# Routing tokens to slots of one expert each in a two-layer transformer kernel on one NeuronCore

## What is computed

```python
xn = _layernorm(x)
probs = softmax(einsum('bsd,ed->bse', xn, Wr))
topv, topi = top_k(probs, 2)
combine = sum(topv[..., None] * one_hot(topi, 8), axis=2)
for e in range(8):                       # w1: 128 x 512, w2: 512 x 128
    h = gelu(einsum('bsd,dh->bsh', xn, w1[e]) + b1[e])
    out += combine[..., e, None] * (einsum('bsh,hd->bsd', h, w2[e]) + b2[e])
x = x + attention0(xn) + out
...
```

## Time and profile before

| | us |
|---|---|
| median of 3 runs (lowest, highest) | 2019.29 (2015.37, 2021.03) |
| the profiled execution's own time | 2017.26 |
| its span in the profile | 2015.5 |
| TensorE busy | 1758.9 (87%) |
| VectorE, ScalarE, GpSimd busy | 1471.3, 1327.4, 654.6 |

### The profile page before, as it was taken

How to read it: one execution, slowest core, us unless ns; L and a number is a source line. 1 busy time by engine, 2 the same in 40 slices (tenths; PEclk the granted TensorE clock), 3 DMA queues, 4 the chain that set the end, 5 groups by cost and what they waited for, 6 DMA issues and landing times. The chain is left out here.

```text
span 2015.5 us, 36012 instructions
## 1 busy us (share of the span) xinstructions
PE 1758.9 (87%) x10163; PEld 1049.0 (52%) x10163; DVE 1471.3 (73%) x4707; ACT 1327.4 (66%) x2819; POOL 654.6 (32%) x1554
## 2 busy tenths in 40 slices
PE   5899999999998897999858889888888838888877
PEld 2455555577776443566524555555555525555544
DVE  5588888311123464888668999999999879999974
ACT  3277777544331522334378999999999839999983
POOL 2154544300002451000044443544354414434440
PEclk8699999999995997999879999999999969999978
DMA  6300000100001221000110110111011101101000
GB/s 163 95 25 20 23 23 16 44 1 0 0 2 49 79 89 42 0 0 0 45 32 17 33 33 17 32 32 32 16 32 32 32 1 32 32 16 32 22 18 15
DMA packets 38186, 61.76 MB, mean 31 GB/s; under 512 B 10226, under 2 KB 15348, under 8 KB 38005
## 3 DMA queue, kind: packets, MB, share of 16 engines
q1 hardware_dynamic: 38069, 60.51, 10.2%
HBM read 34.14 MB, written 17.83 MB: 26 GB/s over the span
## 5 line engine op out<-in xcount | busy, mean ns | idle before, releaser
L1655 ACT ACTIVATE a_trash<-a_sc,a_search 128x1024 bf16<-128x1024 f32 (+7 forms) x768 | 586.1, 767 | 67.4 <-POOL a_search L1591 31.0
L1405 PE MATMUL a_ps_s<-a_k,a_q 128*128 128x512 f32 (+3 forms) x768 | 310.3, 519 | 57.6 <-DVE a_sc L1871 51.5
L1439 PE MATMUL a_ps_o<-a_kT,a_v 128*65 128x512 f32 (+3 forms) x768 | 288.1, 499 | 54.3 <-ACT a_kT L1672 52.7
L1423 PE MATMUL a_ps_t<-g_ident,a_sc 128*128 128x128 f32 x1152 | 227.6, 284 | 19.5 <-ACT a_kT L1672 18.1
L1871 DVE TENSOR_SCALAR_CACHE_REDUCE a_sc<-a_ps_s,g_search 128x1024 f32<-128x1024 f32 (+7 forms) x256 | 207.8, 812 | 25.5 <-PE a_ps_s L1407 17.3
L593 DVE TENSOR_REDUCE a_top<-a_ps_row 128x1 f32<-128x512 f32 (+3 forms) x384 | 196.7, 553 | 26.3 <-PE a_ps_row L431 20.3
L1831 DVE SCALAR_TENSOR_TENSOR a_below<-a_sc,a_found 128x768 f32<-128x768 f32 (+7 forms) x256 | 211.3, 835 | 1.1
L1405 PEld LDWEIGHTS a_ps_s<-a_k,a_q 128*128 128x128 f32 x768 | 131.9, 196 | 153.6 <-issue 93.1
L1425 PE MATMUL a_ps_t<-a_minus,a_short 128*128 128x128 bf16 x1152 | 211.1, 221 | 0.0
L1423 PEld LDWEIGHTS a_ps_t<-g_ident,a_sc 128*128 128x128 f32 x1152 | 164.0, 142 | 90.0 <-ACT a_kT L1672 46.1
L557 ACT ACTIVATE a_prob<-a_ps_col 128x1024 f32<-128x1024 f32 (+7 forms) x256 | 159.2, 650 | 68.9 <-PE a_ps_col L444 65.6
(11 more groups left out here) (267 smaller groups left out, 3382.0 us busy)
## 6 DMA issues: line engine op xcount, KB each, us to landing
a_v<-g_v SPq DMA_DIRECT2D x32, 260.0 KB, 2.3
q1turned<-p_full SPq DMA_DIRECT2D x32, 256.0 KB, 2.0
a_q<-q1turned SPq DMA_DIRECT2D x32, 256.0 KB, 3.6
a_k<-k1turned SPq DMA_DIRECT2D x32, 256.0 KB, 4.0
stack<-p_parts SPq DMA_DIRECT2D x24, 256.0 KB, 3.7
le_q<-stack SPq DMA_DIRECT2D x32, 96.0 KB, 2.2
le_k<-stack SPq DMA_DIRECT2D x32, 96.0 KB, 2.2
le_w<-d_w SPq DMA_DIRECT2D x1, 2048.0 KB, 9.4
```

What stands on the lines that cost most here:

```text
L1405: pe.matmul(ps_s[:, j % 2, c:c + w], q[:, p, i * P:width], k[:, p, c:c + w], start=True, stop=True)
L1423: pe.matmul(out, columns(h, i)[:, c * P:(c + 1) * P], g.ident[:, :], is_transpose=True, start=True, stop=False)
L1439: m = pe.matmul(ps_o[0:VW1, lo // HALF, (lo % HALF) * P:CH], v[:, p, c, :], kT[:, u % 2, a * P:b * P], start=(c == 0), stop=(c == LAST[lo ...
L1655: act.activation(trash[:, u % 2, 0:(i + 1) * P], columns(h, i), ACT.Sign, scale=-1.0, bias=trials[:, p, c, i:i + 1], accum_out=balance[:, ...
```

## The change

Each token takes two experts, so 4096 pairs of token and expert are left. They are sorted by expert into slots of 128 rows; a slot belongs to one expert, and the number of slots, NSLOT = 39, is the most that any routing can need. All 39 are always computed.

The router's matmuls move between the query products, and VectorE picks experts, ranks the tokens and works out each token's two rows (`g.spot`) and each slot's expert (`g.owner`) between its copies of values. In attention, SP first fills a buffer in memory with zeros; GpSimd, in sections 4 to 19, sends each tile of `xn` there twice by indirect DMA, each token's row to its place. In the experts' stage SP reads the slots back, and per slot TensorE transposes the 128 rows, VectorE copies them, GpSimd copies the owner's `w1` to a ring of four buffers, ScalarE takes four Gelus of 128x128, and TensorE reads `w2` at an address from a register. TensorE, ScalarE and GpSimd each load the slot's owner from memory on chip into a register. VectorE copies results, and SP saves three slots at a time. In `project_layer1` GpSimd gathers two rows per token by 32 indirect DMAs, ahead of its memsets, and VectorE adds them times the token's two probabilities. The addition of `g.acc` is gone. GpSimd's sections of attention are written out instead of looped. The four bias operations stand between the slots' copies, after slots 18, 22, 26 and 30.

```diff
+NSLOT = (2 * B * S + NE * (P - 1)) // P
+GS = 3
...
+                pool.memset(taken[:, 0:LEAD, :], 0.0).then_inc(lead_clear, 1)
+                pool.memset(sums[:, :, 0:LEAD, :], 0.0).then_inc(lead_clear, 1)
+                pool.memset(ends[:, :, 0:NE // 2], 0.0).then_inc(lead_clear, 1)
+                pool.memset(g.zero[:, :], 0.0).then_inc(lead_clear, 1)
+                pool.wait_ge(lead_clear, 4)
...
+                def choose():
+
+                    dve.wait_ge(r_ready, 1)
+                    dve.wait_ge(w_in, 16 * 15)
+                    dve.wait_ge(lead_clear, 4)
+                    keep(dve.tensor_copy(g.logits[:, :, :], ps_r[:, :, :]))
+                    keep(dve.tensor_reduce(m1[:, :], g.logits[:, :, :], AX.X, ALU.max))
+                    dve.tensor_tensor(ta[:, :, :], g.logits[:, :, :], wide(m1[:, :]), ALU.subtract).then_inc(exp_in, 1)
...
+                    for x, step_back in enumerate((1, 2, 4, 8)):
+                        b = sums[:, x % 2, :, :]
+                        m = dve.tensor_tensor(b[:, LEAD:LEAD + NT, :], a[:, LEAD:LEAD + NT, :],
+                                              a[:, LEAD - step_back:LEAD + NT - step_back, :], ALU.add)
+                        if x < 3:
+                            keep(m)
+                        a = b
+                        yield
...
+                    dve.tensor_copy(g.spot[:, :, :], at[:, :, :]).then_inc(g.spotted, 1)
...
+                    dve.tensor_copy(g.owner[:, :], owner[:, :]).then_inc(g.spotted, 1)
...
+                work = choose()
+                for t in range(NT):
+                    if t == COUNT_AT:
+                        for _ in work:
+                            pass
+                        work = assign()
+                    keep_v(t)
+                    if t < COUNT_AT:
+                        for _ in range(3):
+                            next(work, None)
...
+                act.wait_ge(exp_in, 1)
+                act.activation(pr[:, :, :], ta[:, :, :], ACT.Exp).then_inc(exp_out, 1)
...
+                    if w == 0:
+                        for t in range(c * (CH // P), (c + 1) * (CH // P)):
+                            last = pe.matmul(ps_r[:, t, :], g.xnT[:, t * P:(t + 1) * P], wr[:, :], start=True, stop=True)
+                        if c == NCQ - 1:
+                            last.then_inc(r_ready, 1)
...
+                    if t == COUNT_AT:
+                        pe.wait_ge(counted, 1)
+                        total = sums[:, 1, LEAD:LEAD + NT, :]
+                        pe.matmul(ps_rank, notabove[:, :], taken[:, LEAD:LEAD + NT, :], start=True, stop=False)
+                        pe.matmul(ps_rank, g.ones[:, :], total, start=False, stop=True)
+                        pe.matmul(ps_count, g.ones[:, :], sums[:, 1, LEAD + NT - 1, :], start=True, stop=True).then_inc(ranked, 1)
...
+                sp.dma_start(g.d_slots.rearrange("(s p) d -> p s d", p=P), g.zero.rearrange(
+                    "p (o d) -> p o d", o=1).broadcast_to([P, NSLOT, D])).then_inc(g.zeroed, 16)
...
+                def send(t, x):
+
+                    pool.indirect_dma_start(g.d_slots[:, :], bass.IndirectOffsetOnAxis(ap=g.spot[:, x, t:t + 1], axis=0),
+                                            g.xn[:, t, :], None, bounds_check=NSLOT * P - 1,
+                                            oob_is_err=False).then_inc(g.sent, 16)
...
+                    if NQ < n <= NQ + NT:
+                        pool.wait_ge(g.sent, 32 * (n - NQ))
...
+                        if NQ <= n < NQ + NT:
+                            for x in range(2):
+                                send(n - NQ, x)
...
-                sections(pool, section)
+                pool.wait_ge(g.spotted, 2)
+                for n in range(-1, NH + 2):
+                    if n == NQ:
+                        pool.wait_ge(g.zeroed, 16)
+                    section(n, n // NQ, n % NQ)
...
+        LOADS = [0, 3, 9, 21, NSLOT]
...
+                sp.wait_ge(g.sent, 16 * 2 * NT)
+                slots = g.d_slots.rearrange("(s p) d -> p s d", p=P)
+                for i, (lo, hi) in enumerate(zip(LOADS, LOADS[1:])):
+                    sp.dma_start(xg[:, lo:hi, :], slots[:, lo:hi, :]).then_inc(slots_in[i], 16)
...
+                    sp.wait_ge(y_kept, (i + 1) * GS)
+                    sp.dma_start(outs[:, i * GS:(i + 1) * GS, :], g.ysb[:, i % 2, :, :]).then_inc(g.y_saved[i % 2], 16)
...
+                for s in range(NSLOT):
+                    at = pool.value_load(g.owner[0:1, s:s + 1], min_val=0, max_val=(NE - 1) * HID)
+                    if s >= NW:
+                        pool.wait_ge(h_ready, (s - NW + 1) * HC)
+                    pool.tensor_copy(own[:, s % NW, :], w1[:, bass.ds(at, HID)]).then_inc(own_ready, 1)
+                    if s == 18:
+                        pool.wait_ge(g.trees_in, 64)
+                        b(pool.tensor_copy(binp[0:1, 0, :], g.bin32[0:1, :]))
...
+                def turn(s):
+                    pe.wait_ge(slots_in[load_of[s]], 16)
+                    if s >= 2:
+                        pe.wait_ge(x_ready, s - 1)
+                    pe.transpose(ps_t[:, s % 2, 0:P], xg[:, s, :], g.ident[:, :]).then_inc(x_turned, 1)
...
+                def hidden(s):
+                    pe.wait_ge(x_ready, s + 1)
+                    pe.wait_ge(own_ready, s + 1)
+                    if s >= 2:
+                        pe.wait_ge(h_read, (s - 1) * HC)
+                    for c in range(HC):
+                        pe.matmul(ps_h[:, s % 2, c * P:(c + 1) * P], own[:, s % NW, c * P:(c + 1) * P], xT[:, s % 4, :],
+                                  start=True, stop=True).then_inc(h_ready, 1)
...
+                def output(s, at):
+                    if s >= 2:
+                        pe.wait_ge(y_kept, s - 1)
+                    for c in range(HC):
+                        pe.wait_ge(h_read, s * HC + c + 1)
+                        m = pe.matmul(ps_y[:, s % 2, 0:P], hid[:, s % 2, c, :], w2[:, bass.ds(at + c * D, D)],
+                                      start=(c == 0), stop=(c == HC - 1))
...
+                for s in range(NSLOT):
+                    if s + 2 < NSLOT:
+                        turn(s + 2)
+                    if s + 1 < NSLOT:
+                        then = owner_of(s + 1)
+                        hidden(s + 1)
+                    output(s, now)
+                    now = then
...
+                for s in range(NSLOT):
+                    first = act.value_load(g.owner[0:1, s:s + 1], min_val=0, max_val=(NE - 1) * HID) // P
+                    if s >= 2:
+                        act.wait_ge(y_ready, s - 1)
+                    act.wait_ge(h_ready, (s + 1) * HC)
+                    for c in range(HC):
+                        act.activation(hid[:, s % 2, c, :], ps_h[:, s % 2, c * P:(c + 1) * P], ACT.Gelu,
+                                       bias=b1[:, bass.ds(first + c, 1)]).then_inc(h_read, 1)
...
-                def chunk(c):
-                    for e in range(NE):
-                        for t in range(TC):
-                            dve.wait_ge(y_ready, c * NE + (e + 1))
-                            if e >= 1:
-                                dve.wait_ge(y_read, (c * NE + (e - 1)) * TC + (t + 1))
-                            a = acc[:, bass.ds(c * CH + t * P, P)]
-                            w = comb[:, bass.ds(c * (TC * NE) + (t * NE + e), 1)]
-                            if e == 0:
-                                m = dve.tensor_scalar(a, ps_y[:, e % 2, t, :], w, None, ALU.mult)
-                            else:
-                                m = dve.scalar_tensor_tensor(a, ps_y[:, e % 2, t, :], w, a, ALU.mult, ALU.add)
-                            m.then_inc(y_read, 1)
...
+                def keep_x(s):
+                    dve.wait_ge(x_turned, s + 1)
+                    if s >= 4:
+                        dve.wait_ge(h_ready, (s - 3) * HC)
+                    dve.tensor_copy(xT[:, s % 4, :], ps_t[:, s % 2, 0:P]).then_inc(x_ready, 1)
+
+                def keep_y(s):
+                    i = s // GS
+                    dve.wait_ge(y_ready, s + 1)
+                    if i >= 2:
+                        dve.wait_ge(g.y_saved[i % 2], 16 * (i // 2))
+                    dve.tensor_copy(g.ysb[:, i % 2, s % GS, :], ps_y[:, s % 2, 0:P]).then_inc(y_kept, 1)
...
-                    dve.tensor_tensor(g.x[:, t, :], g.x[:, t, :], g.acc[:, t, :], ALU.add).then_inc(x1_ready, 1)
...
+                def weigh(t, x, got):
+                    dve.scalar_tensor_tensor(g.x[:, t, :], mixed[x][:, t, :], g.gate[:, x, t:t + 1], g.x[:, t, :],
+                                             ALU.mult, ALU.add).then_inc(got, 1)
+
                 for t in range(NT):
-                    dve.wait_ge(sum_ready, t + 1)
-                    dve.wait_ge(x1_ready, t + 1)
-                    dve.tensor_tensor(g.x[:, t, :], g.x[:, t, :], ps_b[:, t % 2, 0:P], ALU.add).then_inc(acc_ready, 1)
```

(17 more changed lines are left out.)

255 lines of the change are left out of this document (157 added, 98 removed).

## The result

The changed kernel takes 1929.59 us (median of four runs, 1928.07 to 1931.29) against 2020.16 (2015.37 to 2023.96) for the kernel before: ratio 0.9553, 95% interval 0.9531 to 0.9576. The profiled execution took 1928.07 us with a span of 1926.2, against 2017.26 and 2015.5: 89 us less. The forecast was 1915, between 1889 and 1980.

A forecast was written before the change was run, and what follows sets the result against it. TensorE was taken to bound the experts' stage, which pays for token rows. From the profiled 2017.3 us, -113.8 - 2 + 4 + 9.7 = -102.1 gave 1915 us, range 1889 to 1980.

The forecast's parts named there:

- Part 1: Experts' loop: 39 slots at 2.6 us plus start, clock and tail, 112.4 us instead of 226.2, so -113.8 us.
- rival A: Cheap case: TensorE's earlier matmuls may cover the register load, slot 2.1 us, indirect DMA 0.9 or less; 1890 us, chance 0.10.
- Rival D: Experts' stage: GpSimd or ScalarE sets the slot through longer register loads, 3.3 us a slot; 1942 us, chance 0.17.
- Rival C: Experts' loop: the clock stays at its lower level throughout, 4.0 us a slot; 1966 us, chance 0.09.
- Part 2: Routing moved into layer 0's projections: -2 us, between -7 (all hidden) and +5.
- Part 3: Scatters in layer 0's attention: sixteen sections lengthen from 9.00 to 9.6 us, partly absorbed; +4 us, between 0 and +12.
- x: GpSimd's price for issuing one indirect DMA, in attention's scatters and layer 1's gathers: 1.2 us, between 0.43 and 2.2.
- B: Scatters and gathers: each indirect DMA costs GpSimd 2.2 us, a DMA's landing; 1979 us, chance 0.14.
- E: Scatters and gathers: an indirect DMA's price from 2.8 us makes the kernel slower, 2062 us at 3.5; chance 0.06.
- Part 4: Gathers at the start of layer 1: the norm comes after 45.4 us instead of 35.7, +9.7 us.
- The two paths are level: Start of layer 1: sums and weighted additions take 45.3 us, GpSimd's gathers with their last additions 45.4.
- memsets ... hidden by 4 us: Start of layer 1: GpSimd's memsets behind the gathers end at about 52 us, before the first copy of values at 56.

The follow-up runs named there:

- experiments 5 to 7: Changed kernel with layer 1's search repair never taken; TensorE loads the slot's expert zero (no engine reads it), five and three times per slot: 1853.21, 1945.50, 1905.24 us.
- experiment 9: Changed kernel with layer 1's search repair never taken, each scatter in attention sent a second time to unused memory: 1872.14 us.
- experiment 7: Changed kernel with layer 1's search repair never taken, TensorE loading the slot's expert three times per slot instead of once: 1905.24 us.
- experiment 6: Changed kernel with layer 1's search repair never taken, TensorE loading the slot's expert five times per slot instead of once: 1945.50 us.
- experiment 8: Changed kernel with layer 1's search repair never taken, the second choice's sixteen gathers and weighted additions left out: 1840.51 us.

## Why the prediction came out right, and where it was wrong

The time lay in the range and 15 us from the point, but by luck: two errors nearly cancel. Without the second repair the kernel would have taken 1893, and the forecast would have been 22 us too slow.

"No row shows such a load", the ground on which the register load was put at 0.65 us, was wrong: the trace of before has 32 of them on VectorE's queue (least, median and most in ns). They would have given the price, though not the cover.

```profile
L1883 DVEq TENSOR_LOAD <-a_flag x32: 303/526/559, 1060.8 to 1985.2; - x32
```

- **Part 1, -113.8, measured -143.9.** The step that failed is "so I take 0.65 exposed: 2.6 us a slot". The slot is 1.895, of which 39 make 27.5 us of the error; the matmuls were right (1.95). The load itself is as long as thought, 0.62 to 0.64 us, but TensorE has 1.2 to 1.3 us of issued work to cover it (experiments 5 to 7). The lower bound of the term, 0, was the truth, and rival A had named the reason. Start, clock and tail took 8.9 instead of 11.
- **Rival D** (GpSimd or ScalarE sets the slot): no. GpSimd waits 35 us for TensorE in the stage.
- **Rival C** (the clock stays low): no, 1.00 from 385 on, as in the row it was weighed against, and 1.00 in experiment 7 as well. With 2.2 us of idle in a slot at full clock (experiment 6) the clock did go down at times, to a mean of 0.82 over 125 us. The Trainium skill, "TensorE: Matmul & The Clock Gate", section "HAM oscillation", describes such a loss, of a loop whose matmuls wait for data at each step. Here it came with gaps of 2.2 us (experiment 6), and not with those of 0.7 to 0.8 (experiment 7).
- **Part 2, -2, measured -3.4.** Inside its bounds.
- **Part 3, +4, measured +3.5.** Right for the wrong reason. "If nothing held it back, GpSimd's own chain would be ... 7.2" was 1.7 us too long: masks that have queued up run 0.25 apart, not 0.5, and the chain is 5.5 (experiment 9). GpSimd does not bound the section; sections with scatters are about 0.2 us longer (9.16 to 9.22 against 9.00 to 9.16). VectorE's `a_peak` (231 ns instead of 168) is one small part of that; the rest was not followed up.
- **x**: 1.30 us instead of 1.2, inside 0.43 to 2.2, so rivals B and E fall. The estimate behind B, 2.15 us from a formula of the Trainium skill ("DMA: Bandwidth & Descriptors", section "Anatomy of one DMA — SWDGE (gpsimd) path"), is a time to completion, to be held against the 2.6 us from the start of the last gather (504.04) to VectorE's release (506.63); GpSimd itself is free after 1.30.
- **Part 4, +9.7, measured +14.1.** "The two paths are level" failed: the gathers came last by 8 us. They cost 32 x 0.1 more, and one of them took 3.10 us, beside VectorE's weighted additions. The other path was 3 us shorter than its 45.3: the last sum came at 33.4 instead of 35.7 and an addition took 0.26, not 0.3. Experiment 8 shows the bound.
- **"memsets ... hidden by 4 us"**: they end before the first copy of values needs them, as worked out, but the clear holds L98 up by 2.1 us on the way, and with the scaling of weights behind it L101 and L106 take 0.4 and 1.8 longer. The cover was looked for in time only, not in what the two engines share.
- **Not in the sum at all: +37**, the second repair. The section of 63 us, GpSimd's idle of 41.59 us before one `a_reach` and the seven tests of one repair stood in the trace of before. The sum took everything behind the norm as unchanged, which holds of the instructions listed and not of a branch on data that the change alters in its last bits.

## What to carry to other kernels

If a kernel branches on its data, count the branch's executions before and after, and take it out of both to see what a change is worth: here 131 us looked like 91, and a reordered addition came with 37 that it cannot be credited with. Price an instruction that blocks a queue against the work already issued ahead of it, not by its length. Where work is moved under a cover, ask what the two engines share as well as whether it ends in time.
